# Score products of the attention as four 32-row array tiles, one per head, with 24-row stacks

## The reference, cut to what matters

```python
inner = (x @ Wi).reshape(Bb, Tt, Hh, dh).transpose(0, 2, 1, 3)
outer = (x @ Wo).reshape(Bb, Tt, Hh, dh).transpose(0, 2, 1, 3)
alignment = jnp.einsum('bhqd,bhkd->bhqk', inner, outer) / scale
attn_align = jax.nn.softmax(alignment, axis=-1)
attn = attn_align * aperture[..., :, None] * expression[..., None, :]
attn = attn / (attn.sum(axis=-1, keepdims=True) + 1e-08)
converged = jnp.einsum('bhqk,bhkd->bhqd', attn, v)
```

## Time and profile before

| | us |
|---|---|
| median of 3 runs | 519.0 |
| lowest and highest | 518.63, 519.26 |
| span of the profiled execution | 516.1 |
| attention steps with maxima (14) | 177.1 to 366.6 |
| attention steps without (2) | to 391.3 |

### The profile page before, as it was taken

The page is one execution under the profiler, slowest core; times in us unless marked ns, Lnnn a source line. Parts: engine busy times, 40 slices in busy tenths (PEclk is TensorE's granted clock), DMA queues, the critical chain, the costliest instruction groups (busy, mean ns, idle before and its releaser), DMA issues.

```text
span 516.1 us, 7820 instructions
## 1 busy us (share of the span) xinstructions
PE 427.1 (83%) x2252; PEld 250.8 (49%) x2252; DVE 400.4 (78%) x841; ACT 239.9 (46%) x439; POOL 68.6 (13%) x105
## 2 busy tenths in 40 slices
PE   2605999995588899999999999999996506999995
PEld 2501557773454445555555545554553402567773
DVE  6698848899689987778777777777655598768884
ACT  2400443330341267777676777766784201543332
POOL 5510002149000010000000000000002500001100
PEclk9999999998788799999999999999999655999999
DMA  5000012210058810111111111110110000012212
GB/s 166 1 0 1 1 30 62 61 31 0 4 213 276 297 61 25 37 37 43 42 42 42 42 42 42 42 42 1 35 31 0 0 0 2 1 33 59 61 32 81
DMA packets 24749, 26.03 MB, mean 50 GB/s; under 512 B 3634, under 2 KB 16438, under 8 KB 24726
## 3 DMA queue, kind: packets, MB, share of 16 engines
q1 hardware_dynamic: 24726, 25.74, 16.0%
HBM read 16.16 MB, written 9.44 MB: 50 GB/s over the span
## 4 chain that ended last, share of the span: by engine, by line
PE 69%; DVE 25%; issue 3%; ACT 2%; DMA 1%; DVEq 0%; ACTq 0%
PE ps L1133 12%; PE ps L1158 12%; PE ps L1148 10%; DVE neg_max L807 6%; PE ps L999 5%; PE ps L1035 5%; DVE heads_out L707 3%; PE ps L1018 3%; PE ps L1020 3%; PE ps L1019 3%; DVE values L704 3%; PE ps L1050 2%; PE ps L1051 2%; PE ps L960 2%; DVE probs L746 2%
## 5 line engine op out<-in xcount | busy, mean ns | idle before, releaser
L807 DVE TENSOR_REDUCE neg_max<-ps 128x1 f32<-128x512 f32 x256 | 163.4, 684 | 38.9 <-PE ps L1133 38.9
L597 ACT ACTIVATE probs<-ps 128x512 f32<-128x512 f32 x256 | 137.8, 598 | 64.6 <-PE ps L1148 62.9
L1133 PE MATMUL ps<-k_stack,q_stack 128*128 128x512 f32 x256 | 113.7, 452 | 4.8 <-DVE neg_max L807 3.5
L1148 PE MATMUL ps<-q_stack,k_stack 128*128 128x512 f32 x256 | 100.6, 403 | 0.2 <-ACT probs L597 0.2
L1133 PEld LDWEIGHTS ps<-k_stack,q_stack 128*128 128x128 f32 x256 | 49.0, 192 | 68.8 <-DVE neg_max L807 61.7
L1158 PE MATMUL ps<-probs,v_ext 128*32 128x512 f32 x512 | 68.2, 605 | 0.0
L1148 PEld LDWEIGHTS ps<-q_stack,k_stack 128*128 128x128 f32 x256 | 47.7, 190 | 12.7 <-ACT probs L597 5.7
L523 ACT CAST k_stack<-ps 128x512 fp32r<-128x512 f32 x32 | 17.2, 589 | 67.7 <-PE ps L999 67.7
L451 POOL TENSOR_TENSOR w_lo<-w_gu,w_hi 128x512 fp32r<-128x512 f32 x16 | 20.4, 1279 | 149.7 <-ACT w_hi L510 149.7
L769 DVE TENSOR_TENSOR vae_and_gates<-heads_out,ps 128x512 f32<-128x512 f32 x32 | 21.9, 687 | 19.7 <-ACT heads_out L531 17.7
L746 DVE TENSOR_TENSOR probs<-slot_row,slot 128x1024 f16<-128x1024 f16 x32 | 36.5, 1216 | 0.1
(11 more groups left out here) (151 smaller groups left out, 574.8 us busy)
## 6 DMA issues: line engine op xcount, KB each, us to landing
parts_dram<-part_hi SPq DMA_DIRECT2D x8, 512.0 KB, 3.6
parts_dram<-part_lo SPq DMA_DIRECT2D x8, 512.0 KB, 4.9
q_stack<-parts_dram SPq DMA_DIRECT2D x32, 128.0 KB
k_stack<-parts_dram SPq DMA_DIRECT2D x32, 128.0 KB
w_gu<-in_L_ffn_Wg_dram SPq DMA_DIRECT2D x16, 128.0 KB, 2.1
w_gu<-in_L_ffn_Wu_dram SPq DMA_DIRECT2D x16, 128.0 KB, 2.2
wd_sb<-in_L_ffn_Wd_dram SPq DMA_DIRECT2D x16, 128.0 KB, 2.2
x<-in_L_attn_x_dram SPq DMA_DIRECT2D x4, 256.0 KB, 3.8
```

What stands on the lines that cost most here:

```text
L597: nc.scalar.activation(probs[:, u // HG, u % HG, :], ps[:, RING + ring_bank(step, u), :], ACT.Exp, scale=SCORE_SCALE).then_inc(probs_ready, 1)
L807: nc.vector.tensor_reduce(neg_max[:, g, qt, col:col + 1], ps[:, ring_bank(step, u), :], AX.X, ALU.max, negate=True).then_inc(max_taken, 1)
L1133: nc.tensor.matmul(ps[:, ring_bank(step, u), :], q_stack[:, g, pp, chunk(qt)], k_stack[:, g, 2 * pp + jj, :], start=True, stop=True).then_ ...
L1148: nc.tensor.matmul(ps[:, RING + ring_bank(step, u), :], k_stack[:, g, j, chunk(c)], q_stack[:, g, j // 2, :], start=True, stop=True).then_ ...
```

## The change

Each head of a group gets its own 32-partition quarter: rows 32j to 32j+23 hold three pairings of 8 dimensions (lo·lo is dropped), row 32j+24 the maximum (queries) or one (keys). A product addresses only those 24 (maximum) or 25 (score) partitions, so it is emitted as a 32x128 tile of the array at row 32j, where it was one 128x128 product. The units of a maxima step are renumbered so that the tile of a maximum differs from those of the scores beside it: score u uses row tile u mod 4, maximum u tile (u+2) mod 4. `q_stack` and `k_stack` shrink to 512 columns per group; the picked tokens get a buffer of their own, and the placement matrix of even experts moves to `part_lo`. The stored parts are 3 instead of 4 blocks per head.

```diff
-        q_stack = sb("q_stack", [P, G, PAIRS, S], F32R)
-        k_stack = sb("k_stack", [P, G, HG, S], F32R)
+        q_stack = sb("q_stack", [P, G, S], F32R)
+        k_stack = sb("k_stack", [P, G, S], F32R)
+        picked = sb("picked", [P, 2, E, B, K], F32R)
...
+        def max_unit(u):
+            return u // HG, (u + 2) % HG
...
             def load_stacks(b, g):
-                for qk in range(2):
-                    rows = parts_dram[qk].rearrange("b (g pp jj) d a t -> g jj b (d a) pp t", g=G, pp=PAIRS)
-                    for jj in range(2):
-                        at = slice(64 * jj, 64 * jj + 4 * DH)
-                        stack = q_stack[at, g] if qk == 0 else k_stack[at, g].rearrange("r (pp jj) t -> r jj pp t", jj=2)[:, jj]
-                        sp.dma_start(stack.bitcast(F32), rows[g, jj, bass.ds(b, 1)].squeeze(0)).then_inc(stacks_loaded[g], 16)
+                for qk, stack in enumerate((q_stack, k_stack)):
+                    rows = parts_dram[qk].rearrange("b (g j) d a t -> g j b (d a) t", g=G)
+                    for j in range(HG):
+                        sp.dma_start(stack[32 * j:32 * j + ROWS, g, :].bitcast(F32),
+                                     rows[g, j, bass.ds(b, 1)].squeeze(0)).then_inc(stacks_loaded[g], 16)
...
-                for jj in range(2):
-                    sp.dma_start(q_stack[64 * jj + 32:64 * jj + 33, g].bitcast(F32),
-                                 max_rows[2 * jj:2 * jj + 2, g % 2, :].bitcast(F32)).then_inc(max_rows_loaded[g], 16)
+                sp.dma_start(q_stack[ROWS:P:32, g, :].bitcast(F32), max_rows[:, g % 2, :].bitcast(F32)).then_inc(max_rows_loaded[g], 16)
...
-                pool.wait_ge(gate_up_done[0], 2 * MI * E)
-                nc.gpsimd.memset(k_stack[:].bitcast(F32), 0.0).then_inc(pool_consts, 1)
...
             halves(0)
+            nc.gpsimd.memset(k_stack[:].bitcast(F32), 1.0).then_inc(stacks_made, 1)
             affinity_parts(0)
...
             def max_scores(n, step, u):
-                jj, pp = u // C // 2, u // C % 2
+                qt, j = max_unit(u)
+                rows = slice(32 * j, 32 * j + ROWS)
                 pe.wait_ge(max_taken, ring_wait(n, step, u, 3))
-                nc.tensor.matmul(ps[:, ring_bank(step, u), :], q_stack[:, g, pp, chunk(qt)], k_stack[:, g, 2 * pp + jj, :],
+                nc.tensor.matmul(ps[:, ring_bank(step, u), :], q_stack[rows, g, chunk(qt)], k_stack[rows, g, :],
...
                 g, c, j = step % G, u // HG, u % HG
                 pe.wait_ge(probs_ready, ring_wait(n, step, u, 1))
-                nc.tensor.matmul(ps[:, RING + ring_bank(step, u), :], k_stack[:, g, j, chunk(c)], q_stack[:, g, j // 2, :],
+                rows = slice(32 * j, 32 * j + ROWS + 1)
+                nc.tensor.matmul(ps[:, RING + ring_bank(step, u), :], k_stack[rows, g, chunk(c)], q_stack[rows, g, :],
```

More of the change, by code:

```diff
@@ L60, in macaron_block @@
     HG = H // G
-    PAIRS = HG // 2
+    PARTS = 3
+    ROWS = PARTS * DH
     VW = 32
@@ L157, in macaron_block @@
         combinedT = xnT
-        picked_hi, picked_lo = (k_stack[:].rearrange("p (n g) j s -> p n (g j s)", n=2)[:, n].rearrange(
-            "p (e b s) -> p e b s", e=E, b=B) for n in range(2))
+        picked_hi, picked_lo = picked[:, 0], picked[:, 1]
         hidden = vae_and_gates[:, 0:2 * MI * B * K].rearrange("p (u m s) -> p u m s", u=2, m=MI)
@@ L310, in store_parts @@
                     for qk in range(2):
-                        blocks = parts_dram[qk, b].rearrange("h d (m n) t -> m n (h d) t", m=2)
+                        blocks = parts_dram[qk, b].rearrange("h d a t -> (h d) a t")
                         sp.wait_ge(ready, 2 * b + qk + 1)
-                        twice = blocks[half] if qk == 0 else blocks[:, half]
-                        sp.dma_start(twice.rearrange("n r t -> r n t"),
-                                     parts[:, b % 2, qk, :].bitcast(F32).unsqueeze(1).broadcast_to([P, 2, S])).then_inc(stored[b % 2][qk], 16)
@@ L325, in clear_max_rows @@
-            def clear_max_rows(g):
-                for jj in range(2):
-                    sp.dma_start(q_stack[64 * jj + 4 * DH:64 * jj + 4 * DH + 1, g].bitcast(F32), zero_rows_dram).then_inc(stacks_loaded[g], 16)
+                        mine = parts[:, b % 2, qk, :].bitcast(F32).unsqueeze(1)
+                        if half == 1:
+                            at = 2 - qk
+                            sp.dma_start(blocks[:, at:at + 1], mine).then_inc(stored[b % 2][qk], 16)
+                        else:
+                            at = slice(0, 2) if qk == 0 else slice(0, 3, 2)
+                            sp.dma_start(blocks[:, at], mine.broadcast_to([P, 2, S])).then_inc(stored[b % 2][qk], 16)
@@ L1049, in scatter @@
                     for b in range(B):
-                        nc.tensor.matmul(ps[:, b, :], wy_hi[:, u, b, :], place[:, u, b, :], start=False, stop=False, skip_group_check=True)
-                        last = nc.tensor.matmul(ps[:, b, :], wy_lo[:, u, b, :], place[:, u, b, :], start=False, stop=final, skip_group_check=True)
+                        nc.tensor.matmul(ps[:, b, :], wy_hi[:, u, b, :], place[u][:, b, :], start=False, stop=False, skip_group_check=True)
+                        last = nc.tensor.matmul(ps[:, b, :], wy_lo[:, u, b, :], place[u][:, b, :], start=False, stop=final, skip_group_check=True)
                         if final:
```

42 lines of the change are left out of this document (15 added, 27 removed).

## The result

The changed kernel takes 591.41 us (median of 4 runs, 589.55 to 592.15); the kernel before took 519.13 us on the same chip (4 runs, 518.63 to 519.30). The ratio is 1.1395, with a 95% interval of 1.1371 to 1.1418: 72 us slower, where 24 us faster was forecast. The profiled execution took 592.15 us with a span of 590.4. Executions that are over 1.5% longer than the fastest of the same kernel are left out of medians and ratios; in this document that is one run, in experiment 9.

What follows compares the result with a forecast made beforehand. PE was taken to bound the kernel, with DVE next. Full steps save 21.3 us, step 0 0.8 and the two without maxima 1.9: 24.0, less 0.3 for stacks, giving 495 us, range 484 to 510.

Steps and rivals of the forecast that it cites:

- The sum of the forecast: Attention steps with maxima: DVE's reductions 9.65, norm_heads 0.70 and stalls give 11.84 us a step, against 13.48 before.
- The third rival: Attention steps: PE's clock falls to half, 18.6 us a step, priced at 40% of steps, 534 us; chance 0.07.
- the argument against it: Against the falling clock in the steps: whole-array value blocks and transposes fill 5 of 12 us, leaving PE few gaps.
- The overlap: Score and maximum products on PE: neighbours in different row tiles run side by side, pitch 0.11 us in place of 0.23.
- p: Pitch on PE between a score and the maximum behind it: 0.23 us before, taken as 0.11 after.
- DVE as the bound, with stalls behind value blocks: Steps with maxima: DVE becomes the bound, 85 to 90% busy, stalling 0.31 us at k = 3 and 7.
- The fill that goes ended long before its readers: free too: POOL's removed fill: said to gain or cost nothing, since it ended long before its readers.
- The terms of cover: Edits costed at little or nothing: later first stacks lose 0.3 us; other loads hidden, POOL's fills free.
- The stacks' eight loads in place of four: First stacks before the attention: land up to 1.8 us later, a loss between 0 and 1.0, taken as 0.3.
- The fill at its new place: POOL's fill of 2048 columns, where POOL sat idle 3.83 us waiting for DVE's affinity: 1.7 us, free.
- The block of value products, whose change of tile shape: Value blocks on PE in each step: the tiling-mode switch adds nothing; the block starts 0.33 us behind its score, as before.

Runs made afterwards that it cites:

- experiment 9: Kernel with 64-row tiles in pairs, 24-row stacks and early key-stack fill (499.33 us), plus zero products among its first maxima: whole-array 504.59 us, or 64-row 501.51 us.
- experiment 2: Changed kernel with all score and maximum products in the first 32-row tile, so none overlap (only its time counts): 689.61 us, one run.
- experiment 5: Changed kernel with 24 whole-array products directly ahead of the first attention step, so the steps are entered at full clock: 596.73 us, one run.
- experiment 3: Kernel before, its score and maximum products cut to 64-row tiles and maxima reordered so neighbours lie in different halves: 511.01 us, ratio 0.9859.
- experiment 7: Changed kernel with 128-row products (only its time counts), with POOL's late fills put back at their old place: 518.31 us against 506.07 without, one run.
- experiment 1: Changed kernel with every score and maximum product reading all 128 partitions, as one 128x128 product (only its time counts): 506.07 us, one run.

## Why the prediction was wrong

**The step that failed** is the clock. The sum of the forecast, 11.84 us a step, had it at 1.00 in all steps; it was 0.50 throughout the steps with maxima, and such a step took 19.36 us. The third rival had the mechanism, the place and the price: at half clock 18.6 us a step. Had I taken it for all steps, the sum would have been 519 + 14 x (18.6 - 13.48) = 591. That this is the measured time is chance: each step took 0.76 us more, 10.6 in all, and the 12 us ahead of the attention, which I did not have, made up for it. What I wrote of the rival was "PE is then busy all the time, which should bring the clock back, so I price it at 40% of the steps", and a chance of 0.07. The changed kernel has PE busy 95% of the time from 300 to 340 us at 0.50, experiment 2 has it busy 100% at 0.50, experiment 5 shows 1.00 lost under a PE that is hardly idle (3.84 of 4.00 us before it falls, 4.00 of 4.00 while it does). Also wrong was the argument against it, that "value blocks and transposes alone fill 5 of 12 us with the whole array": with them, and with 7 or 16 whole-array fillers on top, the clock stays down. I had read the earlier trace rows as a PE with gaps, and the quarter of the array's rows, which the same paragraph names, decided nothing in it. In experiment 3 PE's gaps are as large (37.88 of 40 us busy, the same as in the changed kernel) at 1.00.

The Trainium skill, "TensorE: Matmul & The Clock Gate", Part 1, explains the clock by how busy PE has been. As the profile counts busy, the runs do not bear this out: experiment 2 is the counterexample. The measurement decides.

**The overlap** was the right mechanism, better than I sized it: p is near 0, not 0.11. At half clock it is worth 98 us against one tile (experiment 2), and that does not pay for the lost clock.

**DVE as the bound, with stalls behind value blocks.** Not so in the changed kernel: DVE is 56% busy. In the 64-row kernel, whose clock holds, a step is 12.58 us with DVE at 85%, against the forecast's 11.84 at p = 0.11. There only two heads lie side by side, so the forecast for four was never put to the test at full clock, and stays open.

**"The fill that goes ended long before its readers: free too"** was the second error, a term put at nothing that was worth 12 us, and in the other direction. I looked for who reads what the fill writes, and not for who is held while it runs. Two lines of DVE with means far above their kind in the trace of before would have told.

**The terms of cover** held. The stacks' eight loads in place of four delay nothing: DVE takes its first sixteen reductions in one row of 9.70 us, without an idle entry. The fill at its new place takes 1.80 us, where I had said 1.7. The block of value products, whose change of tile shape I had put at nothing extra, has its price of before at full clock in experiment 3: it starts 0.32 us behind its score and lets the next maximum start 1.00 later (233.10, 233.42, 234.42), against 0.33 and 1.00.

**The sum as measured:** 519.1 - 12.2 (fill, experiment 7) + 85 (tiles at half clock, experiment 1) = 592, against 591.4.

## What to carry to other kernels

Before products are cut to few rows, price the kernel at half of PE's clock and treat that as a case of its own: in this kernel products of 24 and 25 rows lost it, those of 33 rows lost it for most of the steps, products of 64 rows kept it once it was up, and a PE that is always busy was no protection. Tiles of 64 rows, at full clock, gave 7 us here where four of 32 rows at half clock cost 85. And when a POOL fill goes or moves, look at what DVE does while it runs, at lengths above the usual for the same operation, not only at who reads the filled buffer.

## What the runs showed of the hardware that I had not expected

- In this kernel the granted clock differed with the number of rows that the products read, and not with PE's busy time: the same kernel with the same order ran its steps at 1.00 with 128 rows (506 us, PE busy 39.74 of 40 us), and at 0.50 with 24 and 25 (591 us with up to four at a time, PE busy 37.88; 690 us one by one, PE busy 40.00). Of two kernels with products in the same places, the one reading 64 rows kept 1.00 from about 200 us on (511 us), the one reading 33 went between both levels (572 us, one run). Rows of zeros in `k_stack` were enough for the first of these two, and whole-array products of zeros held 1.00 in experiment 9. That fewer rows are the cause of the lower level in the steps is shown; why, and why 7 or 16 whole-array products a step did not bring it back, is not.
- Four products in different row tiles start within 0.02 us. Behind them the next in the same tiles comes 0.6 us later at half clock.
- Alternating 64-row and 128-row products costs 0.74 us a pair at full clock, with 0.42 and 0.32 to the next start, against 0.23 between whole-array products.
- A POOL memset of 8192 columns (6.93 us), and one of 4096 columns in a single partition (3.6 us, half of 7.24), each hold the DVE cast or placement that starts beside them until the fill has ended: the cast takes 5.88 us in place of 0.43, four placements 7.86 in place of 1.67.
